# Maxima across partitions by a DMA round trip instead of TensorE transposes, and a mixing stage that starts 20 steps earlier

## The reference

```python
xn = layernorm(x)
# 1. graph part: degrees, embeddings by degree, and a sum over edges into their source node
sum3d = segment_sum(edge_attr @ W_sum + b_sum, src)
x = x + (xn + z_in[in_deg] + z_out[out_deg] + sigmoid(cent @ W_cent + b_cent)
            + sigmoid(vor @ W_vor + b_vor) + sum3d)
# 2. mixing: linear attention over all nodes, 8 heads of 64; k and v are normalized per head
x = x + (q @ (k.T @ v) / n) @ w_out + b_out
# 3. mixture of 8 experts, 2 per node: layernorm with the expert's ln_g and ln_b, W1, gelu, W2
x = x + sum(weight * (gelu(xe @ W1[e] + b1[e]) @ W2[e] + b2[e]))
```

## Time and profile before

| | |
|---|---|
| median of 3 runs | 2352.93 us (2350.11 to 2361.64) |
| the profiled execution | 2361.64 us, span in its trace 2359.9 us |
| mean granted TensorE clock | 0.846 of full speed |
| busy in the span | TensorE 74%, GpSimd 65%, VectorE 61%, ScalarE 31% |
| last scatter of the edge phase | begins at 1539.43 us |

### The profile page before, as it was taken

One profiled execution on the slowest core, in us unless ns is written; L12 is line 12 of the kernel. 1 busy time (PEld: TensorE's weight loads), 2 busy tenths in 40 slices (PEclk: granted clock), 3 DMA queues, 4 the chain that ended last, 5 costly groups with the idle time before them and its releaser, 6 DMA issues.

```text
span 2359.9 us, 38011 instructions
## 1 busy us (share of the span) xinstructions
PE 1735.6 (74%) x12869; PEld 1383.5 (59%) x12869; DVE 1451.0 (61%) x3795; ACT 727.5 (31%) x1607; POOL 1545.0 (65%) x1009
## 2 busy tenths in 40 slices
PE   2655544477777777677777777179589999999997
PEld 1333333345454544466566665178478888888886
DVE  2789977778778875233333333069866666666664
ACT  1011111144444444211111111047344433334432
POOL 2888888888888888888888888810034444545442
PEclk9676655579999999688888888589699999999999
DMA  9987777765555444555555554365538888878885
GB/s 301 234 181 172 146 154 151 145 103 75 70 69 75 69 69 69 81 74 78 74 85 79 73 85 65 37 167 168 185 98 271 252 252 244 271 240 259 254 268 157
DMA packets 401454, 348.00 MB, mean 147 GB/s; under 512 B 39304, under 2 KB 323531, under 8 KB 401261
## 3 DMA queue, kind: packets, MB, share of 16 engines
q1 hardware_dynamic: 268492, 266.72, 35.7%
q0 software_dynamic: 132768, 78.84, 28.6%
HBM read 236.69 MB, written 108.76 MB: 146 GB/s over the span
## 4 chain that ended last, share of the span: by engine, by line
PE 27%; DMA 26%; POOL 26%; issue 11%; DVE 7%; SPq 2%; ACT 0%; POOLq 0%; DVEq 0%; ACTq 0%
POOL node_table L1535 25%; DMA node_table<-edge_sums,row_i 19%; PE bank L730 10%; PE bank L744 8%; DMA big<-w_parts 6%; PE bank L687 2%; DVE hotB L871 2%; PE bank L699 1%; PE bank L701 1%; PE bank L522 1%; PE bank L679 1%; DVE hotA L868 1%; SPq L1584 1%; PE bank L716 1%; PE bank L482 1%
## 5 line engine op out<-in xcount | busy, mean ns | idle before, releaser
L1535 POOL DMA_INDIRECT node_table<-edge_sums,row_i x782 | 1256.2, 1606 | 278.9 <-issue 206.4
L482 PE MATMUL bank<-edge_rows,same_node 128*128 128x129 f32 x1564 | 293.0, 336 | 209.3 <-ACT edge_sums L1333 109.0
L1333 ACT COPY edge_sums<-bank 128x387 f32<-128x387 f32 (+1 forms) x261 | 125.0, 479 | 1044.1 <-DMA node_table<-edge_sums,row_i 749.6
L482 PEld LDWEIGHTS bank<-edge_rows,same_node 128*128 128x128 f32 x1564 | 250.5, 238 | 256.8 <-issue 228.1
L1561 POOL DMA_INDIRECT result<-mixw,edge_rows x105 | 167.6, 1596 | 307.1 <-DVE mixw L1290 150.1
L1487 ACT ACTIVATE mixw<-bank,edge_rows 128x256 f32<-128x256 f32 (+1 forms) x456 | 242.7, 550 | 354.9 <-PE bank L730 244.4
L730 PE MATMUL bank<-edge_rows,big 128*128 128x256 f16 (+1 forms) x2736 | 296.9, 269 | 21.6 <-DMA big<-w_parts 20.7
L730 PEld LDWEIGHTS bank<-edge_rows,big 128*128 128x128 f16 x2736 | 251.8, 99 | 61.6 <-DMA big<-w_parts 26.3
L744 PE MATMUL bank<-big 128*128 128x256 f16 x2520 | 284.4, 273 | 1.0 <-issue 1.0
L504 PE MATMUL bank<-hotA,hotB 128*128 128x49 bf16 x1564 | 116.9, 200 | 203.4 <-DVE hotB L871 202.2
L1550 POOL DMA_INDIRECT state<-xn_rows,edge_rows x105 | 116.3, 1107 | 221.5 <-DVE edge_rows L1249 189.8
(11 more groups left out here) (283 smaller groups left out, 2516.9 us busy)
## 6 DMA issues: line engine op xcount, KB each, us to landing
big<-w_parts SPq DMA_DIRECT2D x114, 1024.0 KB, 7.1
edge_rows<-edge_attr SPq DMA_DIRECT2D x130, 384.0 KB, 3.7
big<-L_ffn_W SPq DMA_DIRECT2D x128, 128.0 KB
w_parts<-big SPq DMA_DIRECT2D x64, 256.0 KB, 3.5
node_table<-z_parts SPq DMA_DIRECT2D x20, 640.0 KB, 7.4
node_table<-edge_sums,row_i POOLq DMA_INDIRECT x782
mixw<-node_table SPq DMA_DIRECT2D x96, 128.0 KB, 2.4
edge_rows<-L_ffn_b SPq DMA_DIRECT2D x57, 128.0 KB, 8.1
```

What stands on the lines that cost most here:

```text
L482: ins = e.matmul(ps_sum[:, i * XW:(i + 1) * XW], S[:, g % SRING, i * P:(i + 1) * P], X[:, c // LOAD % XRING, c % LOAD, :], start=True, sto ...
L1535: e.indirect_dma_start(table[t], bass.IndirectOffsetOnAxis(ap=row_i[:, g % ORING, i:i + 1], axis=0), O[:, g % ORING, i, 0:RW], None, compu ...
```

## The change

1. The maximum over partitions goes through DRAM. SP stores `peaks[:, n]` as a row of 128 numbers (new DRAM tensor `peak_rows`) at step 6 of the matrix, waits at step 7 until it has landed, and loads that row into all 128 partitions (`peak_all`). At step 10 VectorE takes the maximum of 128 numbers in each partition straight into `tops`. L561, L554, L1009 and L927 go, with their semaphores; `top_row` is not needed.
2. The same for the maxima of |b1| once: one store of 128x8 numbers, one load of all 1024 into every partition (`b1_all`, in a free part of `big`), one maximum over them. L548, L551, L1000 to L1006 go.
3. Bank 5 is free of this work, so the wait in L579 goes, and `MIX0` is 60 instead of 80. `SIDE_STEPS` is 270 instead of 290, still spread over ticks 8 to 256. The start of the mixing's copy into `big` waits for the reading of `b1_all`.

```diff
@@ -71,7 +71,7 @@
...
 Z0 = NORM_END + 2
-MIX0, MIX_EVERY = NORM_END + 51, 2
+MIX0, MIX_EVERY = NORM_END + 31, 2
 FOLD0 = MIX0 + (TILES - 1) * MIX_EVERY + 9
...
@@ -138,6 +138,8 @@
...
     deg_rows = nc.dram_tensor("deg_rows", (TILES, 2 * P), F16, kind="Internal").ap()
+    peak_rows = nc.dram_tensor("peak_rows", (2 * EXPERTS, P), F32, kind="Internal").ap()
+    b1_peak_rows = nc.dram_tensor("b1_peak_rows", (P, EXPERTS), F32, kind="Internal").ap()
     meta = nc.dram_tensor("expert_meta", (EXPERTS, P, META), F32, kind="Internal").ap()
...
@@ -267,16 +269,12 @@
...
     b1_fold = big[0:EXPERTS, 0:HID]
+    b1_all = big[:, HID:HID + EXPERTS * P]
     offset = sb("offset", [P, KC, EXPERTS * EXPERTS])
...
     peaks = sb("peaks", [P, 3 * EXPERTS])
-
-    top_row = sb("top_row", [P, 2 * EXPERTS])
-    b1_top = sb("b1_top", [P, 1])
-    b1_diag = sb("b1_diag", [P, EXPERTS])
-    ps_peak, ps_top = banks[5][0:1, 0:P], banks[5][:, P:P + 1]
-    ps_b1_peak, ps_b1_top = banks[5][0:EXPERTS, 2 * P:3 * P], banks[5][:, 3 * P:3 * P + EXPERTS]
+    peak_all = sb("peak_all", [P, 2, P])
     tops = sb("tops", [P, 3 * EXPERTS])
...
@@ -541,24 +539,6 @@
...
                 ins.then_inc(b1_turned, 1)
-
-            if at_stage(w, 11, WEVERY, 2 * EXPERTS) == EXPERTS - 1:
-                e.wait_ge(b1_dve, 2)
-                e.wait_ge(w_scaled, scale_ops(EXPERTS - 1) + 1)
-                e.transpose(ps_b1_peak, peaks[:, 2 * EXPERTS:3 * EXPERTS], ident).then_inc(b1_spread, 1)
-            if at_stage(w, 12, WEVERY, 2 * EXPERTS) == EXPERTS - 1:
-                e.wait_ge(b1_dve, 4)
-                e.matmul(ps_b1_top, ones, b1_diag, start=True, stop=True).then_inc(b1_spread, 1)
-            if (n := at_stage(w, 9, WEVERY, 2 * EXPERTS)) is not None:
-                e.wait_ge(peak_top, n + 1)
-                e.matmul(ps_top, ones, top_row[:, n:n + 1], start=True, stop=True).then_inc(peak_spread, 1)
-            if (n := at_stage(w, 7, WEVERY, 2 * EXPERTS)) is not None:
-                e.wait_ge(w_peak, n + 1 + min(n + 1, EXPERTS))
-                if n:
-                    e.wait_ge(w_scaled, scale_ops(n - 1) + 1)
-                if n == EXPERTS:
-                    e.wait_ge(b1_dve, 5)
-                e.transpose(ps_peak, peaks[:, n:n + 1], ident).then_inc(peak_turned, 1)
             if (n := at_stage(w, 5, WEVERY, EXPERTS)) is not None:
...
@@ -575,8 +555,6 @@
...
         if (t := at_stage(v, 8, MIX_EVERY, TILES)) is not None:
-            if t == 0:
-                e.wait_ge(w_scaled, scale_ops(2 * EXPERTS))
             e.wait_ge(mix_ks, 3 * t + 3)
...
@@ -923,8 +901,8 @@
...
         v = scale_ops(n)
-        e.wait_ge(peak_spread, n + 1)
-        e.tensor_copy(tops[:, n:n + 1], ps_top).then_inc(w_scaled, 1)
+        e.wait_ge(peak_load[n % 2], 16 * (n // 2 + 1))
+        e.reduce_max(tops[:, n:n + 1], peak_all[:, n % 2, :], AX.X).then_inc(w_scaled, 1)
         e.wait_ge(w_scaled, v + 1)
...
@@ -955,7 +933,7 @@
...
         e.wait_ge(w_scaled, scale_ops(2 * EXPERTS))
-        e.wait_ge(b1_dve, 5)
+        e.wait_ge(b1_dve, 3)
         e.scalar_tensor_tensor(tops[:, 2 * EXPERTS:3 * EXPERTS], tops[:, 0:EXPERTS], float(DIM),
...
@@ -973,20 +951,18 @@
...
         if u == 0:
-            e.memset(top_row, 0.0).then_inc(ln_dve, 1)
-            e.memset(b1_diag, 0.0).then_inc(ln_dve, 1)
             e.memset(offset, 0.0).then_inc(ln_dve, 1)
...
             e.tensor_copy(b1_t[:, :, 0:HC], ps_kv[0][:, P:P + EXPERTS * HC].rearrange("p (e h) -> p e h", h=HC)).then_inc(ln_dve, 1)
-            e.wait_ge(ln_dve, 4)
+            e.wait_ge(ln_dve, 2)
             e.tensor_scalar(gain_a.bitcast(I32).rearrange("p e k -> p (e k)"),
...
                 e.tensor_copy(offset[:, k, 0:EXPERTS * EXPERTS:EXPERTS + 1], ln_t[:, 1, :, k]).then_inc(ln_dve, 1)
-            e.wait_ge(ln_dve, 8)
+            e.wait_ge(ln_dve, 6)
         w = u - W_TICK0
...
@@ -995,18 +971,10 @@
...
                 vector_scale(e, n)
-            if at_stage(w, 12, WEVERY, 2 * EXPERTS) == EXPERTS - 1:
-                e.wait_ge(b1_spread, 2)
-                e.tensor_copy(tops[:, 2 * EXPERTS:3 * EXPERTS], ps_b1_top).then_inc(b1_dve, 1)
-            if at_stage(w, 11, WEVERY, 2 * EXPERTS) == EXPERTS - 1:
-                e.wait_ge(b1_spread, 1)
-                e.reduce_max(b1_top[0:EXPERTS, :], ps_b1_peak, AX.X).then_inc(b1_dve, 1)
-                e.wait_ge(b1_dve, 3)
-                e.tensor_scalar(b1_diag[0:EXPERTS, :], ident[0:EXPERTS, 0:EXPERTS], b1_top[0:EXPERTS, :], None,
-                                ALU.mult).then_inc(b1_dve, 1)
-            if (n := at_stage(w, 8, WEVERY, 2 * EXPERTS)) is not None:
-                e.wait_ge(peak_turned, n + 1)
-                e.reduce_max(top_row[0:1, n:n + 1], ps_peak, AX.X).then_inc(peak_top, 1)
+            if at_stage(w, 9, WEVERY, 2 * EXPERTS) == EXPERTS - 1:
+                e.wait_ge(b1_peak, 32)
+                e.reduce_max(tops[:, 2 * EXPERTS:3 * EXPERTS], b1_all.rearrange("p (n e) -> p e n", e=EXPERTS),
+                             AX.X).then_inc(b1_dve, 1)
             if at_stage(w, 7, WEVERY, 2 * EXPERTS) == EXPERTS - 1:
...
@@ -1380,7 +1348,7 @@
...
                 e.wait_ge(id_rest, 16 * (CH - 1))
-                e.wait_ge(b1_dve, 1)
+                e.wait_ge(b1_dve, 3)
             if t == W_AT // DIM:
...
@@ -1666,6 +1634,20 @@
...
                     e.dma_start(w_parts[which][ex][:, a:a + WN // 2], high[n % 2][:, a:a + WN // 2]).then_inc(w_high_store[n % 2], 16)
+            if at_stage(w, 8, WEVERY, 2 * EXPERTS) == EXPERTS - 1:
+                e.wait_ge(b1_peak, 16)
+                e.dma_start(b1_all, b1_peak_rows.rearrange("p e -> (p e)").partition_broadcast(P)).then_inc(b1_peak, 16)
+            if (n := at_stage(w, 7, WEVERY, 2 * EXPERTS)) is not None:
+                e.wait_ge(peak_store[n % 2], 16 * (n // 2 + 1))
+                if n >= 2:
+                    e.wait_ge(w_scaled, scale_ops(n - 2) + 1)
+                e.dma_start(peak_all[:, n % 2, :], peak_rows[n].partition_broadcast(P)).then_inc(peak_load[n % 2], 16)
+                if n == EXPERTS - 1:
+                    e.wait_ge(b1_dve, 2)
+                    e.dma_start(b1_peak_rows, peaks[:, 2 * EXPERTS:3 * EXPERTS]).then_inc(b1_peak, 16)
+            if (n := at_stage(w, 6, WEVERY, 2 * EXPERTS)) is not None:
+                e.wait_ge(w_peak, n + 1 + min(n + 1, EXPERTS))
+                e.dma_start(peak_rows[n:n + 1, :].rearrange("o p -> p o"), peaks[:, n:n + 1]).then_inc(peak_store[n % 2], 16)
             if (n := at_stage(w, 0, WEVERY, 2 * EXPERTS)) is not None:
```

More of the change, by code:

```diff
@@ L404, in build_layer @@
     w_looked, w_folded, w_peak = sem("w_looked"), sem("w_folded"), sem("w_peak")
-    peak_turned, peak_top, peak_spread = sem("peak_turned"), sem("peak_top"), sem("peak_spread")
+    peak_store, peak_load = sems("peak_store", 2), sems("peak_load", 2)
     w_scaled, w_high, w_low = sem("w_scaled"), sem("w_high"), sem("w_low")
-    b1_kept, b1_turned, b1_dve, b1_spread = sem("b1_kept"), sem("b1_turned"), sem("b1_dve"), sem("b1_spread")
+    b1_kept, b1_turned, b1_dve, b1_peak = sem("b1_kept"), sem("b1_turned"), sem("b1_dve"), sem("b1_peak_dma")
     meta_dve, meta_store = sem("meta_dve"), sem("meta_store")
```

## The result

The changed kernel takes 2418.58 us in the median (2417.92 to 2424.15) against 2355.15 us for the kernel before (median of 4 runs): ratio 1.0273, 95% interval 1.0242 to 1.0304, some 63 us slower. The forecast was 2356 us and no change.

The account below looks back on a forecast made before the run. GpSimd's 782 consecutive scatters were taken to bound the edge phase. Terms 0 + 1.5 + 0 + 1 + 0.5 = 3 us on the median 2352.93 gave 2356 us, no change (chance 0.73); range 2343 to 2371.

Parts of the forecast that it names:

- What bounds the kernel: Edge phase: as long as GpSimd's 782 scatters, one behind the other; other engines run ahead of them.
- Added DMAs: Matrix stretch: new stores and loads slow the scatters' pace by 0 to 4 us; 1.5 us taken.
- The round trip: Maxima through DRAM, from SP's store to VectorE's use: load lands between 416 and 420 us, before 424.79; cost 0.
- Rival 2: Maxima return late through DRAM and VectorE stalls: 2366 us, needing a trip of 27 us; chance 0.07.
- The removed work: Maximum operations dropped on VectorE and TensorE: both run ahead of the scatters, so worth 0.
- Mixing 20 steps earlier: Side steps: the list still ends at tick 256 and nothing waits for its end, so gain 0.
- rival 1: VectorE becomes the bound where mixing overlaps the matrices: 2368 us; chance 0.12.
- the 1 us for the lead: Mixing-matrix overlap: full VectorE eats the margin of scatters released ahead of GpSimd; 0 to 13 us, 1 taken.
- GpSimd beside a fuller VectorE: Mixing overlap: 69 scatters each up to 0.035 us longer; 0 to 2.4 us, 0.5 taken.
- the three terms: Upper ends of the range's costs: DMAs 4 us, released-scatter margin 13 us, scatter pace 2.4 us.
- rival 3: Scatters beside the matrices get quicker from what is removed or thinned out: 2340 us; chance 0.08.
- the DMA term: The 1.5 us taken for new stores and loads slowing scatters beside the matrices, 4 us at most.

## Why the prediction was wrong

- **What bounds the kernel**: right. GpSimd's row of scatters grew longer by 70.5 us, of 73.0 in all.
- **Added DMAs, the step that failed.** I priced them as a share of the bytes or packets beside them, "at most 2/12 of 1.6, times 16: 4 us", and took 1.5. The loads fit that (ratio 1.0006). The stores cost 2.7%, 63 us, 3.9 us each: they hold up packets of the scatters, and GpSimd waits for the landings. Two things were wrong in it. The nearest row I took for a store's landing was that of wide pieces, 3.5 to 5.5 us; nothing in the trace before showed 4-byte pieces side by side, and I put no bound from above on them. And I priced only the scatters' own length and not their landing. I had read that a scatter waits for the fourth before it, and did not work out the margin of that wait as I did for the row numbers: 4 x 1.97 = 7.9 us from the start of a scatter to its landing, beside the matrices. That row was at its limit now and then already: the landing came last before 78 scatters, nearly always within the usual 0.3 us, and held one up by 1.5 us at most. It was the one that broke.
- **The round trip**: the landing of the store was put at 3.5 to 5.5 us and was 9.7, but the conclusion held. From SP's issue at 358.32 to the load's landing at about 367.71 + 0.32 + 4.5 = 372.5 it is 14 us, less than the 20 that were there, and VectorE waited for none of the 16 loads of `peak_all`; its one wait for a new DMA was 3.3 us, for the maxima of |b1|. Rival 2 did not occur. The some 5 us that the prediction worked out from the Trainium skill ("DMA: Bandwidth & Descriptors", Anatomy of one DMA) are 14 in this trace; the Trainium skill gives that figure for DMAs that GpSimd issues, and SP issues these.
- **The removed work**: worth 0, as said. Without any trip and with the matrix maxima off TensorE, the ratio is 1.0005.
- **Mixing 20 steps earlier**: no gain, as said. The lead held (24.5 us of waits for row numbers), so rival 1 did not occur and the 1 us for the lead was not needed.
- **GpSimd beside a fuller VectorE**: I gave it 0.5 and at most 2.4 us, from 0.035 us a scatter. Between 400 and 550 us the scatters took 0.07 us longer with early mixing, twice that, but the rows above do not tie this to VectorE. Early mixing may cost nothing, the 3.5 us of the two traces or the 8 us of the ratios (0.36 points); the runs don't settle it, and all lie within the 12 us that count as no change. The prediction also told the rule of the Trainium skill ("SBUF — State Buffer", SBUF: two separate sides) too widely: there, two SBUF inputs of VectorE block only a GpSimd operation that reads SBUF.
- **The range**: it was built from the steps I had bounded. The rival that came true, a wait of GpSimd for landings, was not among the four. The range also isn't the sum it names: the three terms alone reach 2353 + 4 + 13 + 2.4 = 2372 us, without the 9 us of spread, and the lower end of 2343 leaves out rival 3 at 2340. Neither comes near 2418.58. The sentence "the DMA term fails if scatters from 100 to 450 us are longer or further apart" is what the trace shows: further apart, not longer.

The Trainium skill ("DMA: Bandwidth & Descriptors", Specifications) says that pieces under 512 bytes are read, modified and written. No run here shows the reading and writing back itself. 4, 16 and 32 bytes all lie under 512, and only 4 bytes side by side were slow, so that by itself the size does not explain it.

## What to carry to other kernels

A transfer is not priced by its bytes: ask what else waits for a landing on the same engines, and by how much that wait is covered. Where one queue bounds a kernel, work out the margin of every wait that it has, not only the one that is interesting for the change. To turn a column of 128 numbers into a row by a store to DRAM, leave room between the pieces (64 bytes from one to the next) or give each 16 bytes or more; or let TensorE do it where it has time. Of these, 64 bytes apart and 16 bytes were run as stores alone, and as a whole round trip only 32 bytes.

## What the runs showed of the hardware

- A store of 128 pieces of 4 bytes side by side in DRAM landed in 9.7 us in the median (9.0 in another run). Scatters under way with it landed 12.1 us after their start in the case shown, and 14.1 at the longest wait (worked out from the waits). With 32 bytes a piece a store landed in 3.6 us.
- Around such stores packets of other transfers took up to 7.4 us; the longest in the kernel before took 2.3.
- Pieces of 4 bytes 64 bytes apart, or of 16 or 32 bytes side by side, cost nothing that could be measured (ratios 0.9994 to 1.0012), and of 4 bytes 512 bytes apart at most 0.5% (1.0025, 1.0005 to 1.0046).
- A second such store right behind the first cost nothing more (1.0252 against 1.0267).
